# An adaLN block on one core: own places for two scratch tiles, x1 of batch 0 on VectorE, LoRA operands prepared in smaller pieces, and gate products and mask sums earlier in the order

## The reference, cut to what matters

```python
mod = (silu(c) @ wmod).reshape(2, 6, 1, 512)           # sa, ca, ga, sb, cb, gb
ga, gb = sign(ga) * max(|ga|, 0.25), sign(gb) * max(|gb|, 0.25)
h = layernorm(x) * (1 + ca) + sa                       # x: 2 x 512 x 512
w = weight where its 32 x 32 block has mask sum > 0, else 0
x = x + ga * (h @ w.T + bias)                          # "x1"
h = layernorm(x) * (1 + cb) + sb
h1 = h @ w1.T + 2 * (h @ A1.T) @ B1.T                  # hidden 1376, LoRA rank 16
h3 = h @ w3.T + 2 * (h @ A3.T) @ B3.T
g = silu(h1) * h3
x = x + gb * (g @ w2.T + 2 * (g @ A2.T) @ B2.T)
```

## Time and profile before

| what | value |
|---|---|
| median of 3 runs | 262.52 us (262.13 to 263.01) |
| the profiled execution, its own time | 261.78 us |
| its span, first to last instruction | 260.0 us |
| TensorE busy | 245.4 us (94%), 1202 matmuls |
| VectorE busy | 130.4 us (50%) |
| ScalarE busy | 84.6 us (33%) |
| GpSimd busy | 65.2 us (25%) |
| mean granted TensorE clock | 0.991 |

### The profile page before, as it was taken

How to read it: one execution, slowest core, us unless ns; L and a number is a source line. 1 busy time by engine, 2 the same in 40 slices (tenths; PEclk the granted TensorE clock), 3 DMA queues, 4 the chain that set the end, 5 groups by cost and what they waited for, 6 DMA issues and landing times.

```text
span 260.0 us, 3334 instructions
## 1 busy us (share of the span) xinstructions
PE 245.4 (94%) x1202; PEld 194.1 (75%) x1202; DVE 130.4 (50%) x210; ACT 84.6 (33%) x140; POOL 65.2 (25%) x76
## 2 busy tenths in 40 slices
PE   7999869897999999999999999999999999999990
PEld 6667656685788888888888878888888888888770
DVE  3558889699779947547546422541122102220145
ACT  2456680471432454654533311011101101010100
POOL 1539665586415103312310000230000000000012
PEclk9999999999999999999999999999999999999996
DMA  6999970011431432143135400056000000000004
GB/s 193 390 372 413 417 303 4 1 43 41 131 111 38 126 122 81 43 121 81 49 115 95 26 3 0 0 29 173 3 0 0 0 3 1 0 0 3 0 0 163
DMA packets 12228, 24.00 MB, mean 92 GB/s; under 512 B 1202, under 2 KB 2354, under 8 KB 12212
## 3 DMA queue, kind: packets, MB, share of 16 engines
q1 hardware_dynamic: 12064, 23.65, 29.7%
q10 hardware_dynamic: 148, 0.14, 0.3%
HBM read 21.16 MB, written 2.10 MB: 89 GB/s over the span
## 4 chain that ended last, share of the span: by engine, by line
PE 71%; DVE 10%; DMA 5%; SPq 4%; issue 4%; POOL 2%; ACT 1%; DVEq 0%; POOLq 0%
PE up_a L1056 23%; PE up_b L1056 23%; PE acc L1070 8%; PE acc L1071 8%; PE acc L1069 8%; DMA lora_raw<-in_lora 5%; SPq L313 2%; PE side L1037 2%; DVE parts L729 1%; DVE wa L739 1%; DVE xt L744 1%; DVE ht_lo L672 1%; DVE hbuf L685 1%; DVE raw L753 1%; PE side L1041 1%
## 5 line engine op out<-in xcount | busy, mean ns | idle before, releaser
L853 DVE TENSOR_TENSOR g<-up_b,g 128x512 f32<-128x512 f32 (+1 forms) x22 | 15.2, 690 | 73.2 <-PE up_b L1056 73.2
L407 POOL TENSOR_TENSOR xt<-work,xt 128x512 f32<-128x512 f32 x5 | 6.8, 1379 | 112.7 <-DVE work L768 112.7
L1070 PE MATMUL acc<-w_lo,g_hi 128*128 128x512 f32 (+1 forms) x88 | 34.7, 395 | 0.0
L1071 PE MATMUL acc<-w_hi,g_lo 128*128 128x512 f32 (+1 forms) x88 | 34.7, 394 | 0.0
L1069 PE MATMUL acc<-w_hi,g_hi 128*128 128x512 f32 (+1 forms) x88 | 34.6, 394 | 0.0
L753 DVE SCALAR_TENSOR_TENSOR raw<-side,raw 128x512 f32<-128x512 f32 (+2 forms) x33 | 21.4, 677 | 25.2 <-PE side L1037 18.6
L621 ACT ACTIVATE g<-up_a 128x512 f32<-128x512 f32 (+1 forms) x22 | 13.1, 597 | 59.6 <-PE up_a L1056 59.6
L626 ACT ACTIVATE g_hi<-g 128x512 fp32r<-128x512 f32 (+1 forms) x22 | 13.9, 634 | 52.9 <-DVE g L853 52.9
L548 ACT ACTIVATE w_hi<-raw 128x512 fp32r<-128x512 f32 (+2 forms) x33 | 20.3, 627 | 25.2 <-DVE raw L753 25.2
L1056 PE MATMUL up_a<-ht_lo,w_hi 128*128 128x512 f32 (+1 forms) x88 | 24.6, 397 | 0.3 <-DVE ht_lo L672 0.2
L1056 PE MATMUL up_a<-ht_hi,w_hi 128*128 128x512 f32 (+1 forms) x88 | 24.4, 398 | 0.4 <-ACT w_hi L548 0.4
(11 more groups left out here) (153 smaller groups left out, 353.1 us busy)
## 6 DMA issues: line engine op xcount, KB each, us to landing
raw<-in_ffn SPq DMA_DIRECT2D x33, 256.0 KB, 2.7
wmod_sb<-in_wmod SPq DMA_DIRECT2D x4, 1024.0 KB, 11.5
xt<-in_x SPq DMA_DIRECT2D x8, 256.0 KB, 8.2
wmod_sb<-in_wmod SPq DMA_DIRECT2D x1, 2048.0 KB, 17.0
out<-xt SPq DMA_DIRECT2D x8, 256.0 KB, 3.0
mask_sb<-in_mask SPq DMA_DIRECT2D x4, 256.0 KB, 9.8
wa<-in_weight SPq DMA_DIRECT2D x4, 256.0 KB, 9.9
lora_raw<-in_lora SPq DMA_DIRECT2D x1, 688.0 KB, 14.2
```

Of the source, the lines that this page charges most:

```text
L853: nc.vector.tensor_tensor(g[0:w], up_b[0:w], g[0:w], ALU.mult).then_inc(g_ready, 1)
L1070: nc.tensor.matmul(acc[t][:], hi, down_lo[j][0:w], start=False, stop=False)
L1071: last = nc.tensor.matmul(acc[t][:], lo, down_hi[j][0:w], start=False, stop=(j == HT - 1))
```

## The change

- `whole(6)` and `whole(7)` write into `g` and `gate_row`, which have no other content then, instead of the two places of `hbuf` (`whole_place`). They wait for no low. low(6) and low(7) read there, and SP's load of the FFN's gate into gate_row waits for low(7).
- add_x1(2) and (3) go from GpSimd to VectorE. weight_low(0) and (1) do too, and `w_by_pool` goes.
- The LoRA operands are cut into six pieces instead of four. Pieces 0 (256 columns of B13: hidden tiles 0 and 1) and 1 (A13, 512 columns) are loaded ahead of the gate's weights and passed on VectorE ahead of whole(4). Pieces 2 (128 columns of A2) and 3 (B2, 1024 columns) are passed where the last two were. Pieces 4 (1120 columns of B13) and 5 (640 of A2) are passed in FFN step 0, behind g_lo(0). Pieces 2 to 5 are loaded behind the FFN's last modulation weights. merge(2) waits for four pieces, spread(2) and merge(6) for all six.
- GpSimd: masked_weight_low(3) ahead of two roots, spread(0) ahead of low(4).
- TensorE: gate_rows(0) ahead of attend(0, 2, 2); mask_blocks(2) and (3) one group of attends earlier; VectorE: mask_sum(3) ahead of mask_weight(2).

The diff, cut; a comment names the engine's list:

```diff
-LORA_CUTS = [(LORA_B13, LORA_A13), (LORA_A13, LORA_A2), (LORA_A2, LORA_COLS), (LORA_B2, LORA_B13)]
-LORA_A = (1, 2)
+LORA_FIRST, LORA_EARLY = 2, 4
+LORA_CUTS = [(LORA_B13, LORA_B13 + 2 * P), (LORA_A13, LORA_A2), (LORA_A2, LORA_A2 + P), (LORA_B2, LORA_B13),
+             (LORA_B13 + 2 * P, LORA_A13), (LORA_A2 + P, LORA_COLS)]
+LORA_A = (1, 2, 5)
-X1_POOL = (2, 3, 4, 5, 6, 7)
+X1_POOL = (4, 5, 6, 7)
-W_POOL = (0, 1)
+        def whole_place(q):
+            return {2 * KT - 2: g, 2 * KT - 1: gate_row}[q][:] if q in (2 * KT - 2, 2 * KT - 1) else hbuf[:, q % 2]
...
# sync
             load_x(1)
+            for n in range(LORA_FIRST):
+                load_lora(n)
             load_mod(GATE_A, SHIFT_F, wmod_ga_loaded)
-            for n in range(len(LORA_CUTS)):
-                load_lora(n)
             load_mod(SHIFT_F, GATE_F, wmod_f_loaded)
             for r in range(3 * HT):
                 if r == 2:
                     load_mod(GATE_F, GATE_F + 1, wmod_gf_loaded)
+                    for n in range(LORA_FIRST, len(LORA_CUTS)):
+                        load_lora(n)
...
# gpsimd
             def spread(j):
-                pool.wait_ge(parts_ready, 1)
+                pool.wait_ge(parts_ready, 1 if j < 2 else len(LORA_CUTS))
...
+            masked_weight_low(3)
             root(T, 2)
             root(T + 2, 2)
-            masked_weight_low(3)
             low(3)
+            spread(0)
             low(KT)
...
-            add_x1(2)
-            add_x1(3)
             root(2 * T, 2)
             root(2 * T + 2, 2)
-            spread(0)
             spread(1)
-            weight_low(0)
-            weight_low(1)
...
# scalar
             gate_size(0)
+            lora_high(1)
...
-            for n in range(1, len(LORA_CUTS)):
+            for n in range(LORA_FIRST, len(LORA_CUTS)):
                 lora_high(n)
...
# vector
             def whole(q):
-                if q - 2 in LOW_DVE:
+                if q not in (2 * KT - 2, 2 * KT - 1):
                     dve.wait_ge(*low_done(q - 2))
-                else:
-                    dve.wait_ge(low_by_pool, q - 1)
-                nc.vector.tensor_scalar(hbuf[:, q % 2], turn_bank(q)[:], one_plus[:, second, k, b:b + 1],
+                nc.vector.tensor_scalar(whole_place(q), turn_bank(q)[:], one_plus[:, second, k, b:b + 1],
...
             mask_on(2)
+            mask_sum(3)
             mask_weight(2)
-            mask_sum(3)
...
-            lora_part(0)
+            for n in range(LORA_FIRST):
+                lora_part(n)
...
             add_x1(1)
+            add_x1(2)
+            add_x1(3)
...
-            lora_part(1)
             centres(2 * T + 2)
...
-            lora_part(2)
-            lora_part(3)
+            for n in range(LORA_FIRST, LORA_EARLY):
+                lora_part(n)
+            weight_low(0)
+            weight_low(1)
             whole(9)
...
                 nc.vector.tensor_tensor(g_lo[s % 2][0:w], g[0:w], f32(g_hi[s % 2][0:w]),
                                         ALU.subtract).then_inc(g_low_ready, 1)
+                if s == 0:
+                    for n in range(LORA_EARLY, len(LORA_CUTS)):
+                        lora_part(n)
...
# tensor
             attend(0, 0, 0)
+            mask_blocks(2)
             attend(0, 0, 1)
-            mask_blocks(2)
             attend(0, 0, 2)
+            mask_blocks(3)
             attend(0, 1, 0)
-            mask_blocks(3)
...
             attend(0, 2, 1)
+            gate_rows(0)
             attend(0, 2, 2)
-            gate_rows(0)
...
             attend_last(1)
-            pe.wait_ge(parts_ready, len(LORA_CUTS))
+            pe.wait_ge(parts_ready, LORA_EARLY)
             merge(2)
```

More of the change, by code:

```diff
@@ L262, in lora_place @@
             return lora_raw[:, lo:hi]
-        def w_done(r):
-            by_pool = sum(x in W_POOL for x in range(r + 1))
-            return (w_by_pool, by_pool) if r in W_POOL else (w_ready, r + 1 - by_pool)
         front = [up_a, up_b, *side]
@@ L379, in low @@
                     pool.wait_ge(*h_done(q))
-                    src, tile = hbuf[:, q % 2], (slice(None), k)
+                    src, tile = whole_place(q), (slice(None), k)
                 else:
@@ L407, in add_x2 @@
                 nc.gpsimd.tensor_tensor(xt[:, b, t], work[:, t], xt[:, b, t], ALU.add).then_inc(x2_by_pool, 1)
-            def weight_low(r):
-                src, high, low_part = weight_parts(r)
-                pool.wait_ge(w_high_ready, r + 1)
-                nc.gpsimd.tensor_tensor(low_part, src, f32(high), ALU.subtract).then_inc(w_by_pool, 1)
             def masked_weight_low(k):
@@ L525, in whole @@
                 bias_col, scale = columns_of(q)
-                nc.scalar.activation(hbuf[:, q % 2], turn_bank(q)[:], ACT.Identity, bias=bias_col, scale=scale
+                nc.scalar.activation(whole_place(q), turn_bank(q)[:], ACT.Identity, bias=bias_col, scale=scale
                                      ).then_inc(h_ready, 1)
@@ L671, in low @@
                 dve.wait_ge(*h_done(q))
-                nc.vector.tensor_tensor(ht_lo[b][:, k], hbuf[:, q % 2], f32(ht_hi[b][:, k]), ALU.subtract
+                nc.vector.tensor_tensor(ht_lo[b][:, k], whole_place(q), f32(ht_hi[b][:, k]), ALU.subtract
                                         ).then_inc(low_by_dve, 1)
@@ L1063, in down @@
                 pe.wait_ge(g_low_ready, s + 1)
[L1064 removed]
+                pe.wait_ge(w_ready, 3 * j + 3)
                 if j == 0:
```

8 lines of the change are left out of this document (4 added, 4 removed).

## The result

The changed kernel takes 259.02 us (median of 4 runs, 258.55 to 260.58) against 262.50 of the kernel before: 3.5 us less, ratio 0.9876 with a 95% interval of 0.9832 to 0.9921. 260.1 was predicted, with a range of 258.9 to 262.0. The median lies 0.1 us inside that range, and outside the band of 259.3 to 260.9 that had most of the chances. The direction was right, and so were four of the five steps in kind; the gain was 3.5 us instead of 2.4.

The account below looks back on a forecast made before the run. TensorE, busy throughout from 66.88 to 252.20 us, was the bound, so only its earlier waits could shrink. Terms 0.85 + 1.65 + 0.1 + 0.6 - 0.8 = 2.4 us took 262.5 to 260.1, range 258.9 to 262.0.

Parts of the forecast that it names:

- Step A: Gate of batch 1: earlier gate products and no collision with masked_weight_low(3) start the spread 0.85 us earlier.
- Step B: Last wholes before batch 1's bias products: shorter LoRA pass and no waits for lows; gain grows to 2.5 us.
- Step C: x1 and the way to turn(8): `gates_f` or norms replace the b13 wait, adds about even; gain 2.6 us.
- 0.3 off the chain: Way to turn(8): lora_part(1) no longer runs beside the second root, whose first instruction shortens, saving 0.3 us.
- Step D: VectorE from turn(8) to merge(4): fewer LoRA columns and no low collision, against two weight_lows; gain 3.2 us, 0.6 more.
- Step E: Late LoRA pieces in FFN step 0: a new 0.8 us wait before merge(6) lowers the gain to 2.4 us.
- whole gain: Rival: no wait before merge(6) and a gate load in time, gain 3.2 to 3.6, 258.9 to 259.3 us; chance 0.14.
- Half: Rival: gate and wholes gain, but VectorE before merge(4) costs 1.2 us; 261.4 typical, 261.9 at the end; chance 0.15.
- Slower, by the port: Rival: four adds of x1 each wait for a whole GpSimd low, taking 7.8 us; kernel 264.7 us; chance 0.04.
- Slower, by the queue: Rival: two small transfers ahead of the gate's weights cost about 2 us each beyond their bytes; 263.9 us; chance 0.03.
- No change: Rival: waits of merge(0) and whole(7) only pass on to `gates_f`, with VectorE no earlier; chance 0.04.

Follow-up runs that it names:

- e_gate_late: Changed kernel with gate_rows(0) back behind attend(0,2,2): 258.70 us.
- e_gate_mwl_late: Changed kernel with gate_rows(0) back behind attend(0,2,2) and masked_weight_low(3) back behind the two roots: 258.78 us.
- e_again: Changed kernel run once more without any edit, for an undisturbed profile: 258.72 us.
- e_places_alone: Kernel before the change with one part alone, whole(6) and whole(7) writing to g and gate_row: 260.49 us, ratio 0.9948.
- e_spread_late: Changed kernel with spread(0) back behind the roots of x1, directly ahead of spread(1): 258.90 us.
- e_x1_gpsimd: Changed kernel with the adds of x1 for tiles 2 and 3 back on GpSimd, behind low(7): 259.07 us.
- e_hbuf_shared: Changed kernel with whole(6) and whole(7) back in the two shared places of hbuf, waiting for low(4) and low(5): 260.02 us.
- e_lows_gpsimd: Changed kernel with weight_low(0) and weight_low(1) back on GpSimd: 259.14 us.

## Why the prediction was right, and where its sizes were off

**Step A** put a gain of 0.85 down to the earlier gate products and to the collision with masked_weight_low(3), and wrote the mask pieces off as "at most a short wait". The gain at the transposes is 1.27 (30.90 against 32.17), and at the spread 1.6. The earlier products are worth nothing (e_gate_late). The collision did go, 1.29 to 0.29, but with both moves undone the kernel is as fast, to 0.1 us, so the account was incomplete: the mask work, alone or with the short LoRA pieces, is enough, since it lets the moments of batch 1 start 1.26 earlier. I looked only at the wait of TensorE that mask_blocks(3) ended (0.18 us), not at the waits of 1.67 and 0.49 us that VectorE had for the block sums. By the estimate at e_gate_mwl_late the collision's end alone could have brought some 0.9 of it; that was not run. The gate's weights were to land at 26.2, a new wait of a quarter us. In e_again they land at 25.4 (issued at 13.29, 12.1 to landing), as early as before, and cost nothing; in four other profiles they ended waits of 0.39 to 0.93.

**Step B** was right: bias products 2.74 earlier (2.5 forecast), with ScalarE's highs as the pace and 0.80 us of the wait left (0.6 forecast). The extra comes from step A; the part's own gain is 1.47, as e_places_alone has it too (1.46; 1.65 forecast). All of it is the wholes' waits for lows; the shorter LoRA pass, named beside them, gave nothing there.

**Step C** was right in kind: `gates_f` takes b13's place, and four adds cost what two did. The term "0.3 off the chain" was right as well (in e_again 0.23 for the first root instruction, not 0.56), but I then took 0.1 for the whole step where 0.4 came. e_spread_late and e_x1_gpsimd bear out that neither the b13 wait nor the adds' move is worth anything by itself. The estimate for the adds, 3.2 beside one low, measured 3.09. The four adds take 2.48 with no low beside them (e_hbuf_shared) and 3.09 with the one that runs until 38.39 (e_again): the overlap costs 0.61. That agrees with the port rule of the Trainium skill (SBUF — State Buffer, "Who interferes with whom"), by which I had estimated 0.6 to 1.3.

**Step D** is the term that was mis-sized most, 0.6 for 1.15 at merge(4). Its own working gave 0.9, and I took 0.6 because ScalarE and TensorE might bound it. As far as the rows show they don't: the stretch from the end of `gates_f` to the end of merge(2) took 11.84 us before (51.08 to 62.92) and 10.70 now (47.93 to 58.63), 1.14 less, with VectorE busy throughout, as this window of e_again shows:

```profile
47.93:58.63 10.70, 9.83 (x51) 8.21 (x51) 10.70 (x17) 5.35 (x8) 3.01 (x4) 1.00 0.14 51
```

By rows, the passes went from 2.25 to 1.54, the lows from 2.76 to 1.28, and 1.29 came in: 0.9, and 0.24 that I can't assign. e_lows_gpsimd splits it: with the weight lows on GpSimd the stretch is 10.93 (48.72 to 59.65), so 0.9 of the 1.1 comes with the 640 columns put off, and a quarter us with the weight lows' move.

**Step E** was right to a tenth: merge(6) waits 0.63, and TensorE's lead falls from 4.3 to 3.5, by the 0.8 of the forecast.

So the sum of 2.4 lacked 0.4 in A, 0.3 in C and 0.5 in D, against 0.2 too much in B. **Rivals**: "whole gain" named 258.9 to 259.3, and the median fell there, but not for its reason, since the wait at merge(6) did come. What brought the median there is that A, C and D each gave more than their terms, of which it named only part of A; that it hit was luck. "Half" rested on VectorE's stretch getting longer; it got shorter. "Slower, by the port" needed three lows left at the adds; one was, ending at 38.39. "Slower, by the queue" fell with the landing at 25.4 behind two small transfers: the fixed 2.0 us that the Trainium skill gives for a DMA (DMA: Bandwidth & Descriptors, "Anatomy of one DMA") does not add up in a filled queue here: twice 2 us beyond the bytes would have been a landing near 30, and the latest in any profile was 26.9. "No change" fell with merge(6) 3.5 us earlier.
